# DLRM tower on one core: one compare for both features of a unit instead of one for each

## The reference

```python
e = jnp.stack([tbl_0[ids[:, 0]], ..., tbl_31[ids[:, 31]]], axis=1)   # 2048 x 32 x 128
z = einsum('bfd,bgd->bfg', e, e), of which the 496 pairs f < g are kept
h = jnp.concatenate([z, dense_ctx], axis=1)                          # 2048 x 512
h = jnp.maximum(h @ W_top1 + b_top1, 0.0)                            # 512 x 512
h = jnp.maximum(h @ W_top2 + b_top2, 0.0)                            # 512 x 256
y = h @ W_top3                                                       # 256 x 1
```

## Time and profile before

| | |
|---|---|
| time, median of 3 | 439.18 us (438.72 to 439.19) |
| the profiled execution: its time, its span | 440.8 us, 438.9 us |
| mean granted TensorE clock | 0.984 |
| PE, DVE, POOL busy | 90%, 77%, 70% of the span |

### The profile page before, as it was taken

The page is one execution under the profiler, slowest core; times in us unless marked ns, Lnnn a source line. Parts: engine busy times, 40 slices in busy tenths (PEclk is TensorE's granted clock), DMA queues, the critical chain, the costliest instruction groups (busy, mean ns, idle before and its releaser), DMA issues.

```text
span 438.9 us, 11697 instructions
## 1 busy us (share of the span) xinstructions
PE 396.6 (90%) x4672; PEld 371.2 (85%) x4672; DVE 337.4 (77%) x873; ACT 121.7 (28%) x220; POOL 307.6 (70%) x324
## 2 busy tenths in 40 slices
PE   0469677999999999999999999999999999999967
PEld 0468577989999889989999989999999999998866
DVE  3789949999498958899498949899589949891510
ACT  1254410133213321233113321233214311332323
POOL 5777877777777777777777777777777777777100
PEclk9998998899999999999999999999999999999999
DMA  6999953435234332424332442436332543332000
GB/s 131 235 240 215 218 174 80 104 78 100 77 83 77 99 98 57 99 75 103 74 81 72 106 93 58 97 79 100 73 86 72 102 93 66 89 74 54 21 3 2
DMA packets 31374, 42.11 MB, mean 96 GB/s; under 512 B 11164, under 2 KB 24220, under 8 KB 31352
## 3 DMA queue, kind: packets, MB, share of 16 engines
q1 hardware_dynamic: 18936, 20.64, 22.7%
q0 software_dynamic: 10240, 20.99, 18.9%
q10 hardware_dynamic: 2176, 0.17, 0.4%
HBM read 41.77 MB, written 0.01 MB: 95 GB/s over the span
## 4 chain that ended last, share of the span: by engine, by line
PE 55%; DVE 28%; issue 6%; DMA 5%; SPq 3%; ACT 1%; DVEq 0%; ACTq 0%
PE sel_ps L295 19%; DVE onehot L628 17%; PE gram_ps L314 12%; PE work_ps L352 11%; DVE pairs L639 9%; PE work_ps L360 6%; DMA pairs<-tables_selected 5%; PE work_ps L277 3%; PE work_ps L425 2%; SPq L227 1%; SPq L222 1%; DVE table_lo L662 1%; PE work_ps L434 1%; PE work_ps L331 1%; DVE pairs L653 1%
## 5 line engine op out<-in xcount | busy, mean ns | idle before, releaser
L248 POOL DMA_INDIRECT gathered<-table,tile_ids x320 | 307.4, 960 | 100.3 <-issue 95.4
L628 DVE TENSOR_SCALAR onehot<-id_rows,row_no 128x256 fp32r<-128x256 int32 x768 | 238.8, 386 | 19.4 <-DMA id_rows<-ids_selected 12.2
L295 PE MATMUL sel_ps<-onehot,table_hi 125*128 125x256 f32 x768 | 202.0, 300 | 30.1 <-DVE table_lo L662 23.1
L295 PE MATMUL sel_ps<-onehot,table_lo 125*128 125x256 f32 x768 | 194.5, 290 | 0.0
L295 PEld LDWEIGHTS sel_ps<-onehot,table_hi 125*128 125x128 f32 x768 | 152.1, 198 | 38.8 <-DVE table_lo L662 24.0
L295 PEld LDWEIGHTS sel_ps<-onehot,table_lo 125*128 125x128 f32 x768 | 152.7, 199 | 0.0
L639 DVE STREAM_TRANSPOSE pairs<-gram_ps 32x1024 f32<-32x1024 f32 x60 | 74.8, 1246 | 56.0 <-PE gram_ps L314 55.3
L487 ACT ACTIVATE rows_T<-sel_ps 128x512 f32<-128x512 f32 x48 | 30.0, 627 | 127.3 <-PE sel_ps L295 91.9
L314 PEld LDWEIGHTS gram_ps<-rows_T 128*64 128x64 f32 x1920 | 57.5, 138 | 7.2 <-issue 7.2
L478 ACT ACTIVATE rows_T<-work_ps 128x512 f32<-128x512 f32 x80 | 45.5, 599 | 61.1 <-PE work_ps L277 61.1
L314 PE MATMUL gram_ps<-rows_T 128*64 128x64 f32 x1920 | 59.6, 223 | 2.4 <-issue 2.4
(11 more groups left out here) (26 smaller groups left out, 84.1 us busy)
## 6 DMA issues: line engine op xcount, KB each, us to landing
id_rows<-ids_selected SPq DMA_DIRECT2D x48, 256.0 KB
gathered<-table,tile_ids POOLq DMA_INDIRECT x320
pairs<-tables_selected SPq DMA_DIRECT2D x6, 448.0 KB
x<-tables_selected SPq DMA_DIRECT2D x6, 448.0 KB
w_sb<-w SPq DMA_DIRECT2D x1, 1024.0 KB
w_sb<-w SPq DMA_DIRECT2D x1, 512.0 KB
pairs<-tables_selected SPq DMA_DIRECT2D x6, 52.0 KB
x<-tables_selected SPq DMA_DIRECT2D x6, 52.0 KB
```

The source lines that it names most:

```text
L248: nc.gpsimd.indirect_dma_start(gathered[:, t, g, :], None, tables_gathered[g], bass.IndirectOffsetOnAxis(ap=slot_id, axis=0)).then_inc(chu ...
L295: last_op = nc.tensor.matmul(sel_ps[:, u % 2, e, :], part[0:SEL_P, 2 * u + e, k, :], onehot[0:SEL_P, (2 * u + h) % HALF_SLOTS, kk, e, :], ...
L628: last_op = nc.vector.tensor_scalar(onehot[:, (2 * u + h) % HALF_SLOTS, kk, e, :], id_rows[:, slot, e, :], row_no[:, k:k + 1], None, ALU.i ...
```

## The change

The loop over the two features of a unit goes; one instruction writes both. `onehot[:, slot, kk]` and `id_rows[:, slot]` are each contiguous over the two features, so the operands become plain runs of 512 columns. Values, buffers, semaphores and the order of all work stay the same.

```diff
                     for kk in range(K_HALF):
                         k = h * K_HALF + kk
-                        for e in range(2):
-                            last_op = nc.vector.tensor_scalar(onehot[:, (2 * u + h) % HALF_SLOTS, kk, e, :],
-                                                              id_rows[:, slot, e, :], row_no[:, k:k + 1], None,
-                                                              ALU.is_equal)
+                        last_op = nc.vector.tensor_scalar(
+                            onehot[:, (2 * u + h) % HALF_SLOTS, kk, :, :].rearrange("p e s -> p (e s)"),
+                            id_rows[:, slot, :, :].rearrange("p e s -> p (e s)"), row_no[:, k:k + 1], None,
+                            ALU.is_equal)
                     last_op.then_inc(onehot_ready, 1)
```

## The result

| | before | after |
|---|---|---|
| median, range | 438.95 us (436.78 to 439.19) | 464.61 us (460.85 to 469.50) |
| ratio | | 1.055, 95% interval 1.049 to 1.061 |
| the profiled execution: time, span | 440.8, 438.9 | 460.85, 458.9 |
| mean gather | 960 ns | 1045 ns |
| end of the last gather | 408.1 | 435.3 |

The medians are of four executions each; the ratio leaves out the one of 469.50 us, which fell in a slower state of the chip.

What follows compares the result with a forecast made beforehand. TensorE was taken to bound the kernel, with GpSimd's gathers close behind. Span 438.9 plus D 10.0, minus margin 6.5, minus 0.2 gave 442.2, or 444.1 as that execution's time; less 1.6 to the median, 442.5, range 436 to 448.

Steps and rivals of the forecast that it cites:

- GpSimd as the second bound, with a margin of 6.5 us: At the kernel's end: gains elsewhere bring it forward at most 6.5 us; gathers later by D move it by D - 6.5.
- A wide compare costs 0.397: On VectorE: a 512-column compare takes 0.397 us in place of two of 0.262, saving 49 us over 384.
- A gather waits until the next VectorE instruction would start: 0.04 us after its start a gather wants something; if a VectorE instruction holds it, the gather waits for the next one's start.
- D: Total by which wide compares make the gathers later: 10.9 us at random phases less 0.9 paid today, 10.0 (bounds 5.6 and 18).
- both rhythms: Compares against gathers: today's harmless lock, next start 0.01 ahead of a gather, and a harmful one, 0.14 ahead, delaying it 0.22.
- Runs of 4 or 8 that break up with waits for id_rows: On VectorE: wide units last 3.3 us, id_rows loads 5.1, so about nine runs a pair, each at a new phase.
- Rival A: Gathers are slowed no more than today, by locking or an equally short hold: 432.7 us, or 436.7 with D = 4; chance 0.19.
- Rival B: On VectorE: the wide compare saves nothing, costing 0.524 us, and the time stays 439.2; chance 0.08.
- Rival C: Long runs lock at a bad phase, 128 gather waits of 0.22, 28 us, time 460; chance 0.11 including what lies between.

Runs made afterwards that it cites:

- the half change: Half 0 of every unit with 512-column compares, half 1 narrow as in the kernel before; 448.79 us, 1.025 of the kernel before.
- the kernel with one wide half in a pair: Kernel before, with 512-column compares only for unit 3 half 1 of each pair after the first; 438.53 us beside 438.67, 0.999.
- three-row form: Changed kernel with compare output laid out as 3 rows of 168, source one run of 504; 447.52 us, 1.020 of the kernel before.
- 384 + 128: Kernel before with each 512 columns cut 384 + 128 instead of 256 + 256; mean gather 962 ns, run only on a chip with late instructions.
- 496 + 16: Kernel before with each 512 columns cut 496 + 16 instead of 256 + 256; 436.25 us, 0.995 of the kernel before.

## Why the prediction was wrong

- **GpSimd as the second bound, with a margin of 6.5 us.** Right. In the profiled executions of the changed kernel, its repeat, the half change and the kernel with one wide half in a pair, the span ends 23.6, 24.1, 24.3 and 24.2 us after the last gather; 24.3 followed from the earlier trace rows.
- **A wide compare costs 0.397.** Right: 0.395.
- **A gather waits until the next VectorE instruction would start.** Right as the first of two meetings. In the three-row form the wait is gone although the compare is wider than the one before and longer than the changed one.
- **"With starts at random against a gather's period ... D = 10.0 us".** This is the step that failed. D was 27.2. First, it knew one moment at which a gather wants the path; there are two, and the second, up to 0.1 us for a compare, showed no cost in the rows of before, because the narrow compares are over by then; the first meetings alone came to about 16 us after the first pair. Second, it averaged over random phases. The phases are not random. A held compare is let go at a fixed place in a gather, so that the next one starts 0.13 ahead of the next gather; where that one is wide, the gather is delayed, and four wide compares fit the lengthened gather of 1.58. Where two compares and two more fit with their hold into a gather's 1.25 us (256 + 256, 384 + 128, 496 + 16), the cost stays near nothing. I had written down both rhythms, and gave the harmful one 0.11 because I expected "a gather's own hold pushes late compares to just ahead of the next gather, as today". It pushes them to 0.13 ahead, where a wide compare does harm, and not to 0.01.
- **Runs of 4 or 8 that break up with waits for id_rows.** They do (29.1 us of waits, 20 times), and it does not protect: a run that begins half a us into a gather is held at once and meets the next gather, as in the rows from 250.97.
- **Rival A** (the wait does not grow): fell. **Rival B** (nothing saved on VectorE): fell. **Rival C** (bad phase) had the right beginning: a held compare, the next one 0.14 ahead of the next gather, a first wait of 0.22. It lacked the second meeting and the repeat over four compares. That its price of 28 us is near the 27.2 is partly luck: it had 128 meetings of 0.22 in the whole kernel, where after the first pair there are 65 such cases of 0.29 on average.

## What to carry to other kernels

Before making a VectorE instruction wider, ask what else issues work beside it. Where GpSimd issues indirect DMAs back to back, look at single gathers in the timeline next to the VectorE instruction that begins just ahead: one lengthened gather tells of a shared path, and the distance between starts tells whether the two fit. Fewer instructions can then be slower (464.6 us here), and a useless-looking cut, 496 + 16, can avoid the loss (436.3). If two engines issue at fixed distances and hold each other up, work out where a held instruction is let go and what the next one then meets, not an average over phases.

## What the runs showed of the hardware

- Compares of 128x512 from int32 to fp32r cost 0.395 us from start to start; laid out so that source and output have different numbers of rows (one of 504, three of 168), 0.645. The fast form delays gathers and is held by them, the slow one is not (99 of 278 gathers against 2 of 276). The Trainium skill (VectorE: DVE Perf Modes, section "Mode 2×_2P — use both read ports for one tensor") says that a single-source instruction in SBUF uses a second port when the outermost sizes of source and output are even, or odd and equal; both forms agree with it.
- A gather can be met twice: 0.04 us after its start, and again by a compare that goes on beyond 0.74 (gathers of 145.02 and 171.03). A compare that would begin between these is held and the next one starts about 1.11 after the gather's start (rows from 250.97 and 173.55). The Trainium skill (SBUF — State Buffer, section "SBUF: two separate sides") has an exclusive lock held for the whole instruction. The runs show less than that at a compare's start: one that begins 0.01 ahead of a gather, or 0.03 ahead of the first meeting (171.04), costs the gather nothing there.
- On three of five chips the same kernel took 627 to 637 us instead of 439, with TensorE's instructions late for no visible reason and a mean granted clock of 0.82 to 0.86, while kernels with half the gathers ran in 428 and 444 on one of these. The cause stays open.
